# Moving two scan products and one copy in a fused FFN, scan and FFN kernel

## The reference

```python
def ffn(x):                       # 128 -> 512 -> 512 -> 512 -> 128, ternary weights, a scale per output
    h = silu(tlin(x, w1)) * tlin(x, w2)
    h = gelu(tlin(h, h1)); h = gelu(tlin(h, h2))
    return tlin(h, w3)

def attn(x):                      # a recurrence over the 512 positions of each of the 8 sequences
    xB = einsum('bsd,dn->sbn', x, B)              # 16 states
    step: h = tanh(xB[t] + h @ A.T)
    y = einsum('sbn,nd->bsd', hs, C)
    return y @ W_out.T + b_out

x = x + 0.5 * ffn(layernorm(x))
x = x + attn(layernorm(x))
x = x + 0.5 * ffn(layernorm(x))
```

## Time and profile before

| | |
|---|---|
| median of 3 runs | 380.41 us (380.18 to 380.73) |
| the profiled execution: its own time, its span | 380.9 us, 378.9 us |
| PE busy | 373.1 us (98% of the span), 1767 products |
| PEld busy | 296.4 us (78%) |
| DVE busy | 280.9 us (74%) |
| ACT busy | 261.1 us (69%) |
| POOL busy | 178.2 us (47%) |
| PE's share of the chain that ended last | 92% |

### The profile page before, as it was taken

How to read it: one execution, slowest core, us unless ns; L and a number is a source line. 1 busy time by engine, 2 the same in 40 slices (tenths; PEclk the granted TensorE clock), 3 DMA queues, 4 the chain that set the end, 5 groups by cost and what they waited for, 6 DMA issues and landing times.

```text
span 378.9 us, 6501 instructions
## 1 busy us (share of the span) xinstructions
PE 373.1 (98%) x1767; PEld 296.4 (78%) x1767; DVE 280.9 (74%) x711; ACT 261.1 (69%) x606; POOL 178.2 (47%) x162
## 2 busy tenths in 40 slices
PE   7999999999999999999999999999999999999996
PEld 5778777778878787878778788878888888887775
DVE  5978988887787877677868866777767677686723
ACT  3899485677758668676685767858576775756655
POOL 3645265675646658342551623525334352433521
PEclk9999999999999999999999999999999999999999
DMA  7920010102001020000001000010000101000010
GB/s 233 434 114 1 28 57 28 58 2 83 3 28 56 2 83 0 28 1 29 29 2 55 1 29 29 2 55 0 37 19 0 55 0 55 0 30 28 1 35 29
DMA packets 7807, 16.66 MB, mean 44 GB/s; under 512 B 1888, under 2 KB 3040, under 8 KB 7520
## 3 DMA queue, kind: packets, MB, share of 16 engines
q1 hardware_dynamic: 7200, 16.10, 11.5%
q10 hardware_dynamic: 576, 0.21, 0.2%
HBM read 9.99 MB, written 2.12 MB: 32 GB/s over the span
## 4 chain that ended last, share of the span: by engine, by line
PE 92%; DMA 2%; DVE 2%; ACT 2%; issue 1%; POOL 1%; SPq 1%; POOLq 0%; ACTq 0%
PE F L291 75%; PE FR L291 7%; DMA w_raw<-in_h1T 2%; PE F L544 2%; PE FR L319 1%; PE SC L439 1%; PE MI L319 1%; PE MI L299 1%; PE FR L309 1%; PE SC L454 1%; PE SC L291 1%; DVE xnt_f L833 1%; PE MI L461 0%; ACT w_hi L1425 0%; DVE u L844 0%
## 5 line engine op out<-in xcount | busy, mean ns | idle before, releaser
L291 PE MATMUL F<-y_hi,w_hi 128*128 128x512 f32 (+1 forms) x484 | 197.0, 407 | 0.3 <-DVE y_lo L1080 0.2
L291 PE MATMUL F<-y_lo,w_hi 128*128 128x512 f32 (+1 forms) x484 | 188.4, 390 | 0.0
L291 PEld LDWEIGHTS F<-y_hi,w_hi 128*128 128x128 f32 x484 | 91.0, 188 | 23.9 <-issue 5.8
L1253 ACT ACTIVATE y<-F,sc 128x512 f32<-128x512 f32 x111 | 76.0, 685 | 42.7 <-PE F L291 41.9
L291 PEld LDWEIGHTS F<-y_lo,w_hi 128*128 128x128 f32 x484 | 91.2, 188 | 15.3
L874 DVE TENSOR_TENSOR y_lo<-y,y_hi 128x512 fp32r<-128x512 f32 x79 | 66.5, 842 | 39.7 <-ACT y_hi L1256 39.7
L1538 POOL TENSOR_TENSOR y_lo<-y,y_hi 128x512 fp32r<-128x512 f32 x48 | 66.6, 1393 | 58.9 <-DVE y_hi L861 48.0
L1544 POOL TENSOR_TENSOR y_lo<-y,y_hi 128x512 fp32r<-128x512 f32 x48 | 62.7, 1314 | 34.7 <-ACT y_hi L1256 34.5
L1256 ACT ACTIVATE y_hi<-F,sc 128x512 fp32r<-128x512 f32 x111 | 75.9, 684 | 0.0
L1272 ACT ACTIVATE h<-SC 128x32 fp32r<-128x32 f32 x96 | 18.8, 195 | 49.2 <-PE SC L454 48.2
L291 PE MATMUL F<-xn_hi,w_hi 128*128 128x512 f32 x118 | 49.5, 419 | 0.0
(11 more groups left out here) (177 smaller groups left out, 438.4 us busy)
## 6 DMA issues: line engine op xcount, KB each, us to landing
w_raw<-mr_row SPq DMA_DIRECT2D x5, 512.0 KB, 3.5
x_all<-in_xT SPq DMA_DIRECT2D x1, 2048.0 KB, 16.5
x_all<-x1c SPq DMA_DIRECT2D x8, 256.0 KB, 2.2
x_all<-lnin SPq DMA_DIRECT2D x8, 256.0 KB, 2.2
out<-outb SPq DMA_DIRECT2D x7, 256.0 KB, 2.0
x_all<-in_xtok SPq DMA_DIRECT2D x1, 1536.0 KB, 12.1
w_raw<-in_h1T SPq DMA_DIRECT2D x2, 512.0 KB, 7.5
w_raw<-in_h2T SPq DMA_DIRECT2D x2, 512.0 KB, 9.0
```

Source lines behind the costliest of these rows:

```text
L291: mm = nc.tensor.matmul(out, wtile(w, layer, k, m), y, start=first and i == 0, stop=last and i == len(pairs) - 1)
L1253: nc.scalar.activation(y23[:, m, :], bankt[:, :], ACT.Gelu, scale=s)
```

## The change

Three things are moved, and nothing is added or left out of what is computed.

1. In the loop of the second half's turns (k = 2 to 5, the new flag `ahead`) PE issues step 0 directly behind the attention's products, and step 1 directly behind `front_tokens`. DVE takes step 0 behind `attention` and step 1 behind the statistics, ahead of the result of layer 4.
2. So that step 0 finds its bank filled, ACT copies `xb_all` for the next turn (`following`) near the end of a turn, ahead of the last `gelu3`. ACT takes steps 0 and 1 one after the other ahead of the first gelu. Turns 1 and 5 stand outside ACT's loop for that.
3. In the first mixed tile PE issues the last product of the first pass behind block 1 of layer 1, next to the transpositions of `to_features("m")`, where it stood ahead of block 1.

```diff
                 layer1(g + 1, 0, gen)
+                layer1(g + 1, 1, gen)
                 first_pass(7)
-                layer1(g + 1, 1, gen)
                 to_features("m", xnt_m, MI, mid)
...
                 def opening(i):
                     if att is not None and i == 1:
                         attention(att[0], att[1])
+                        if ahead:
+                            step(0)
                     if i == 2:
                         if joined:
                             layer4(g - 1, gen)
                         front_tokens(g + 1)
+                        step(1 if ahead else 0)
                 layer2(g, 0, gen, opening)
-                step(0)
                 layer2(g, 1, gen)
-                step(1)
+                if not ahead:
+                    step(1)
...
                 if att is not None:
                     attention(att[0], att[1])
+                if ahead:
+                    step(0)
                 low1(g)
                 front_stats(g + 1)
+                step(1 if ahead else 0)
                 if joined:
                     layer4(1, g - 1, k - 1)
-                step(0)
-                step(1)
+                if not ahead:
+                    step(1)
...
-                if scan is not None:
+                if scan is not None and not ahead:
                     inject(scan[0], scan[1])
                 step(0)
+                if ahead:
+                    step(1)
                 gelu2(g, 0)
-                step(1)
+                if not ahead:
+                    step(1)
...
                 layer1(g + 1, 3)
+                if following is not None:
+                    inject(following[0], following[1])
                 gelu3(g, 3)
```

More of the change, by code:

```diff
@@ L649, in last_results, with turn @@
                 last_layer4(g, r, gen)
-            def turn(k, g, gen, att, scan, joined=True):
+            def turn(k, g, gen, att, scan, joined=True, ahead=False):
                 def step(t):
@@ L705, in round_ @@
                 with pe.Fori(2, CHUNKS - 2) as k:
-                    turn(k, gb + k + CHUNKS, gen, (gb + k + 1, k + 1), (n + k + 2, k + 2))
+                    turn(k, gb + k + CHUNKS, gen, (gb + k + 1, k + 1), (n + k + 2, k + 2), ahead=True)
                 loc = pe.mark_branch_hint_location() if isinstance(r, int) and not gen else None
@@ L1032, in middle_turn, with turn @@
                 end_turn(g)
-            def turn(k, g, att, scan, joined=True):
+            def turn(k, g, att, scan, joined=True, ahead=False):
                 def step(t):
@@ L1190, in round_ @@
                 with dve.Fori(2, CHUNKS - 2) as k:
-                    turn(k, gb + k + CHUNKS, (gb + k + 1, k + 1), gb + FIRST_PASS + k + 2)
+                    turn(k, gb + k + CHUNKS, (gb + k + 1, k + 1), gb + FIRST_PASS + k + 2, ahead=True)
                 if isinstance(r, int):
@@ L1365, in middle_turn, with turn @@
                 gelu3(g, 3)
-            def turn(g, scan):
+            def turn(g, scan, ahead=False, following=None):
                 def step(t):
@@ L1504, in round_ @@
                     turn(gb + CHUNKS, (n + 2, 2))
-                with act.Fori(1, CHUNKS - 2) as k:
-                    turn(gb + k + CHUNKS, (n + k + 2, k + 2))
+                turn(gb + 1 + CHUNKS, (n + 3, 3), following=(n + 4, 4))
+                with act.Fori(2, CHUNKS - 3) as k:
+                    turn(gb + k + CHUNKS, (n + k + 2, k + 2), ahead=True, following=(n + k + 3, k + 3))
+                k = CHUNKS - 3
+                turn(gb + k + CHUNKS, (n + k + 2, k + 2), ahead=True)
                 turn(gb + 2 * CHUNKS - 2, None)
```

## The result

The changed kernel takes 380.86 us (median of 22 runs, 380.49 to 381.45) where the kernel before takes 380.48 (22 runs beside them): a ratio of 1.0013, 95% interval 1.0007 to 1.0019. That is 0.38 us, or 0.13%, slower: little, but the whole interval lies above 1. The forecast was 380.8. The profiled execution takes 381.28 us where it took 380.9.

A forecast was written before the change was run, and what follows sets the result against it. TensorE's string of products was taken to bound the kernel, so only cheaper places or removed waits gain time. Turns -0.24 plus mixed tile +0.63 made +0.39 us on 380.41, or 380.8 us, range 379.9 to 381.4.

The forecast's parts named there:

- the turns: Loop turns k = 2 to 5: 0.06 us gained in each, four times, -0.24 us in all.
- the mixed tile: First mixed tile: moving the last first-pass product delays chains on DVE and ACT, +0.63 us once; bounds +0.48 and -0.06.
- Step costs: TensorE in the loop turns: steps 0 and 1 each cost 0.11 us in their new places; neither saved.
- The chain's gain: Loop turns, from statistics through POOL's `rs_f` to the normalisation and its transpositions' loads: 0.16 us shorter, 4.38 to 4.22.
- slower rival: Loop turns: step 0 is paid ahead of the chain and nothing comes back; +0.11 us a turn, 381.5 us; chance 0.14.
- each turn 0.06 shorter: Loop turns: TensorE's waits fall from 0.21 to 0.15 us a turn, step 1's wait mostly replaced by the normalisation's.
- the bound set there: Sign for the loop turns: the forecast is wrong if the turns differ by more than 0.15 us each.
- L319's wait: Loads of the normalised tile's transpositions into `FR` wait for `xnt_f`; stretch around step 2 1.10 us, was 1.04.
- Turn 1: Second half's turn 1: step 0 moves by one input block, worth nothing; step 1's wait for `h` stays.
- the mixed tile hides its step: Rival: DVE and ACT idle time covers the mixed tile's step, which gains 0.06; turns gain 0.24; 380.1 us; chance 0.17.
- all waits go: Rival: all waits go and steps are cheap beside short products; turns gain 1.08 us in all, 379.3 us; chance 0.07.

The follow-up runs named there:

- the experiment that gained 0.25: Kernel before with step 0 directly behind the transpositions L309 in all turns, on VectorE ahead of layer 4's result: 380.24 us, ratio 0.999; five turns 0.25 us shorter.

## Why the prediction was right, and where it wasn't

- **The total** came out: +0.38 us between the medians (0.27 to 0.72 by the interval), forecast +0.39. Its terms did not, so the agreement to 0.01 is luck. In the trace the turns are 0.27 us above their forecast and the mixed tile 0.08 below, which leaves +0.58; the profiled executions show +0.4 because the one after has 0.13 less at its start and 0.04 less outside the two stretches, and the interval of the medians holds either. What held is that the mixed tile loses about half a microsecond and that the turns don't give it back.
- **Step costs** were right: 0.11 behind the attention's products, which the trace before had not shown. The Trainium skill says that loads of 128 columns in a type that isn't FP32 run at about double speed ("TensorE: Matmul & The Clock Gate", "Weight-path perf modes — Fast Weight Load (FWL) and DoubleRow"). By that the prediction worked out 0.05 for this place, as an estimate; the 0.11 measured shows no such gain for these weights. The rows list their loads as f32, so they may be of the kind that the rule leaves out.
- **The chain's gain, 0.16 us, is the step that failed.** I added a release of 0.05, taken from VectorE to TensorE, to POOL's end. The row shows 0.13 from POOL to VectorE, in all four turns of the loop within 0.01. 2.97 to 2.89 is 0.08 (0.07 at the load), below the 0.11 that step 0 costs ahead of it. The prediction had named this as the point from which its slower rival decides: the turns took that rival's mechanism, at 0.11 - 0.07 = 0.04 each (the loop turns differ by 0.01 to 0.05), not its full 0.11. So "each turn 0.06 shorter" is refuted, and the bound set there (0.15 a turn) was too wide to catch it.
- **The 0.13 is not a latency between POOL and VectorE.** Outside the loop the same pair is 0.03 apart (341.49 to 341.52). Turn 6 of the kernel before:

```profile
340.48 1.01 POOL L1533 TENSOR_TENSOR rs_f<-ve_f,mhalf 128x4 f32<-128x4 f32 x1
...
341.52 1.37 DVE L833 TENSOR_SCALAR xnt_f<-FR,mv_f,rs_f 128x128 f32<-128x128 f32 x4 [0.77 <-POOL rs_f L1533]
```

The normalisation has two semaphores to wait for. In turn 6 its own instruction carries the wait for `rs_f`. In the loop a register operation ahead of it carries that wait (a line that these views leave out): in turn k = 3 of the changed kernel it starts at 274.62, 0.04 behind POOL's end, and the normalisation 0.09 behind that. All kernels here show it in the four turns of the loop and not in turn 6. So the release itself was no longer than I had put it, and the operation between was overlooked; no run takes it away.
- **L319's wait** was read right as what comes next: 1.05 us there, forecast 1.10. With the 0.16 ahead of block 2, TensorE's waits of a turn are 0.26, forecast 0.15.
- **The wait for `outb`** was missing. I moved step 1 ahead of the result of layer 4 on VectorE's queue and looked only at who waits for step 1, not at who waits for `outb` behind it. It cost nothing as long as the chain sets the stretch.
- **Turn 1** was forecast at nothing, with its wait for `h` kept. The wait went and the turn is 0.08 us shorter (22.36 to 22.28): step 0 stands one input block earlier there too, and that is the edit of the experiment that gained 0.25.
- **The mixed tile**: layer 3's load was forecast at 163.33, the tanh at 162.58, and the kernel with this edit alone has both to the digit. L439 was forecast 0.10 too late there (its load at 164.61, measured 164.51). It was taken to wait for the copy in the kernel before. There the copy is this row:

```profile
163.26 0.58 ACT L1268 COPY xn<-MI 128x512 f32<-128x512 f32 x1
```

It ends at 163.84, and L439 loads at 163.98, 0.14 later. After a true wait it is 0.04 to 0.06 (163.89 + 0.58 = 164.47 and 164.51 in the kernel with this edit alone). And in the tile ahead, where the copy was over 8 us before, L439 stands 0.32 behind the start of the product before it (149.13 and 149.45); here it is 0.33 (163.65 and 163.98), where the prediction had reckoned with 0.23. So TensorE was there last, the releaser of the row was only the last semaphore, and nearly 0.10 us of ACT's delay was covered. The reason given against "the mixed tile hides its step", that ACT's chain had no slack, was wrong by that much.
- **ACT's queue keeps its order.** The Trainium skill's "strict FIFO" ("TensorE: Matmul & The Clock Gate", "Architectural detail: the array is 16× 32×32, not 1× 128×128") agrees: `th` starts behind the small tanh in every kernel in which it is queued there (162.64 behind 162.56), and ahead of it in the two in which it is queued ahead (161.95 and 161.58, the small tanh at 162.58 and 162.21). It decided less than thought, since layer 3's stall alone gives +0.49 (L439 at 5.09).
- **Rivals.** "The mixed tile hides its step" is refuted by L439, 0.55 us later, and "all waits go" by the turns, which gained nothing. The slower rival held in kind and not in size.

## What to carry to other kernels

A short step is not free where it stands ahead of the start of a chain that another engine's work comes back from; ask on which side of the chain's start it lands, and gain by starting the chain earlier, not by giving its end more room (other waits follow on the end). An edit that takes a wait from such a chain gives back only what the chain itself gets shorter, to the next releaser and what stands between it and the instruction: in a loop that can be a register operation that carries the wait. And a row's releaser is proof of a wait only if the start follows the releaser's end by that pair's usual distance.

## What the runs showed of the hardware

A waiting instruction that carries the wait itself started 0.03 us behind POOL's end on VectorE (341.49 to 341.52), and a weight load 0.04 to 0.05 behind the end on ACT or VectorE (164.47 to 164.51, 274.04 to 274.09). Where a register operation carried the wait, in the loop, the instruction behind it started 0.13 behind POOL's end (274.59 to 274.72), and 0.21 to 0.22 behind VectorE's with two such operations in between (278.12 to 278.33). A step of 32 columns costs TensorE 0.11 us behind two products of 256 columns, as it does among products of 512, and 0.12 behind four transpositions ahead of a product of 512.
